# Attention sum of a graph network: one operand of the VectorE comparison is read from a bank of TensorE's memory

## The reference

```python
hp = jnp.einsum('nf,hfo->hno', h, w)
e = a_src[:, src] + a_dst[:, dst] + fc_b[0]
e = jax.nn.leaky_relu(e, negative_slope=0.2)
seg_max = jax.ops.segment_max(e.T, src, num_segments=n)
e = jnp.exp(e - seg_max.T[:, src])
seg_sum = jax.ops.segment_sum(e.T, src, num_segments=n)
att = e / seg_sum.T[:, src]
msg = att[:, :, None] * hp[:, dst, :]
agg = jax.vmap(lambda m: jax.ops.segment_sum(m, src, num_segments=n))(msg)
out = agg.mean(axis=0) + bias
```

## Time and profile before

| | |
|---|---|
| median of three runs | 31319.55 us (31306.85 to 31346.87) |
| profiled execution, its own time | 31347.26 us |
| its span | 31345.4 us |
| the stage's loop in it | 18986.3 to 21439.9 us, first to last start of `onehot` |
| busy in the loop (18986 to 21440 us) | PE 1739.85, DVE 2330.63, ACT 495.32, POOL 915.55 us |
| TensorE's granted clock in the loop | 0.62 of full speed (1.0 is 2.4 GHz, 0.5 is 1.2 GHz) |

### The profile page before, as it was taken

The page is one execution under the profiler, slowest core; times in us unless marked ns, Lnnn a source line. Parts: engine busy times, 40 slices in busy tenths (PEclk is TensorE's granted clock), DMA queues, the critical chain, the costliest instruction groups (busy, mean ns, idle before and its releaser), DMA issues. The chain is left out here.

```text
span 31345.4 us, 606960 instructions
## 1 busy us (share of the span) xinstructions
PE 25548.6 (82%) x149627; PEld 16798.5 (54%) x149628; DVE 18784.1 (60%) x47074; ACT 4500.2 (14%) x12240; POOL 16699.4 (53%) x16857
## 2 busy tenths in 40 slices
PE   8777776666678888858999986675888888888888
PEld 6444442222248888826777766664444444444444
DVE  9211115666653333325666668997777777777777
ACT  4111111111110000011111111221111111111111
POOL 0677777777767777716777763332333333333332
PEclk9555555555555555556665565656999999999999
DMA  2111112222221111113333355443332333333222
GB/s 65 34 30 30 30 30 50 51 51 50 51 38 25 25 25 25 25 14 74 79 79 77 80 71 107 124 124 81 70 71 70 71 70 71 71 71 72 71 70 64
DMA packets 2615644, 1869.03 MB, mean 60 GB/s; under 512 B 1600556, under 2 KB 2081066, under 8 KB 2613815
## 3 DMA queue, kind: packets, MB, share of 16 engines
q1 hardware_dynamic: 1914438, 1424.41, 18.6%
q0 software_dynamic: 516000, 217.22, 6.8%
q10 hardware_dynamic: 184400, 220.54, 2.8%
HBM read 1621.01 MB, written 238.82 MB: 59 GB/s over the span
## 5 line engine op out<-in xcount | busy, mean ns | idle before, releaser
L2027 POOL DMA_INDIRECT rows_x<-x_table,index x3125 | 3022.1, 967 | 6780.0 <-DMA index<-in_src 6018.0
L1295 POOL DMA_INDIRECT rows<-x_table,index x3625 | 3445.4, 950 | 2025.7 <-issue 1254.1
L162 PE MATMUL banks<-rows,onehot 128*128 128x33 f32 (+1 forms) x14440 | 3417.0, 413 | 1058.5 <-issue 586.6
L547 POOL DMA_INDIRECT rows<-x_table,index x3125 | 3021.7, 967 | 1853.5 <-DMA index<-in_src 927.2
L162 PEld LDWEIGHTS banks<-rows,onehot 128*128 128x128 f32 x14440 | 3186.1, 328 | 1366.1 <-issue 1357.0
L905 POOL DMA_INDIRECT bucket_pairs<-pair,place_int x3125 | 3150.0, 1008 | 1275.6 <-issue 1213.5
L696 POOL DMA_INDIRECT rows<-x_table,index x3125 | 3142.5, 1006 | 1019.6 <-issue 952.0
L1891 PE MATMUL banks<-first,same_unit 128*128 128x384 f32 (+1 forms) x10000 | 3503.3, 476 | 0.0
L1205 DVE CUSTOM_DVE_ANT_0 junk<-banks,mask 128x320 f32<-128x320 f32 x5800 | 2551.1, 486 | 1563.1 <-PE banks L1240 1540.7
L1760 DVE TENSOR_TENSOR second<-banks,h 128x384 f32<-128x384 f32 (+1 forms) x5000 | 2309.6, 485 | 1068.7 <-PE banks L1891 1015.0
L1879 PE MATMUL banks<-u_turned,w_tensor 32*128 32x384 f32 (+1 forms) x10000 | 2119.5, 501 | 530.9 <-DVE first L1752 530.7
(11 more groups left out here) (395 smaller groups left out, 39498.7 us busy)
## 6 DMA issues: line engine op xcount, KB each, us to landing
key_row<-key_rows SPq DMA_DIRECT2D x1450, 320.0 KB
h<-hidden_dram SPq DMA_DIRECT2D x10000, 40.0 KB
key_row<-dst_rows SPq DMA_DIRECT2D x625, 320.0 KB, 3.4
rows<-x_table,index POOLq DMA_INDIRECT x9875
a_dram<-a ACTq DMA_DIRECT2D x625, 160.0 KB
a<-a_dram SPq DMA_DIRECT2D x625, 160.0 KB
rows_dram<-rows ACTq DMA_DIRECT2D x725, 90.0 KB
x_rows<-rows_dram SPq DMA_DIRECT2D x725, 90.0 KB
```

The costliest lines, as they stand in the source:

```text
L162: mm = nc.tensor.matmul(m["ps"][7][:, 0:width], m["onehot"][j % 3][:, t * P:(t + 1) * P], rows[:, t, :], start=t == 0, stop=t == T - 1)
L547: nc.gpsimd.indirect_dma_start(out=m["rows"][j][:, t * W:t * W + F], out_offset=None, in_=m["x_table"], in_offset=bass.IndirectOffsetOnAxi ...
L1295: nc.gpsimd.indirect_dma_start(out=m["rows"][j][:, t * XA:t * XA + F], out_offset=None, in_=m["x_table"], in_offset=bass.IndirectOffsetOnA ...
L2027: nc.gpsimd.indirect_dma_start(out=m["rows_x"][j][:, t * F:(t + 1) * F], out_offset=None, in_=m["x_table"], in_offset=bass.IndirectOffsetO ...
```

## The change

A copy of the table `ramp` is made once, at the stage's start, in the first 128 columns of bank 3. The comparison of L1339 reads this copy and no longer the one in SBUF. Its other operand, `keys`, and its output stay in SBUF. No instruction moves.

```diff
+    ramp = lambda: m["ps"][3][:, 0:P]
+
...
     def hot_dve(dve, i, j):
         g = SLOTS * i + j
-        nc.vector.tensor_tensor(cut(m["onehot"][j][:, :], t=T), rep(m["keys"][:, bass.ds(T * g, T)], 2, P), rep(m["ramp"][:, :], 1, T),
+        nc.vector.tensor_tensor(cut(m["onehot"][j][:, :], t=T), rep(m["keys"][:, bass.ds(T * g, T)], 2, P), rep(ramp(), 1, T),
                                 ALU.is_equal).then_inc(s["hot"], 1)
...
             link = Chain(dve, s["step"])
             link(nc.vector.memset(m["acc"][:, :], 0.0))
+            link(nc.vector.tensor_copy(ramp(), m["ramp"][:, :]))
```

## The result

The changed kernel takes 30640 us in the median of four runs (30599.45 to 30681.72), the kernel before, on the same chip, 31331 us (31306.85 to 31346.87): a ratio of 0.978 (95% interval 0.9763 to 0.9797), 2.2% faster. The forecast was 30650 us. The profiled execution took 31345.4 us of span before and 30629.5 after, 715.9 us less. Of these the attention sum's loop gives 2453.6 - 1771.9 = 681.7 us (forecast 670); the loop began 18986.3 - 18932.8 = 53.5 us earlier and what lies behind it took 19.3 us more (9924.8 in place of 9905.5), in code that is the same; no run here explains these two, and single executions of the changed kernel lie up to 82 us apart.

A forecast was written before the change was run, and what follows sets the result against it. VectorE, busy 95% of the attention sum's loop, was taken as the bound. 2454 - 626 - 149 + 7 + 98 = 1784 us for the loop, a saving of 670, gave 30650 us in all; range 30530 to 30930.

The forecast's parts named there:

- The wait and its size: Attention sum's loop: the comparison `onehot` stops waiting for GpSimd's multiply in four groups of five, 580 x 1.08 = 626 us saved.
- Rival B: A comparison with one operand in a bank is still kept waiting; nothing changes, 31320 us; chance 0.06.
- rival C: The bank can't be read at speed beside TensorE's writes; `onehot` stretches, costing 341 us: 31660 us; chance 0.02.
- The price of the bank: Reading one operand of the comparison from a PSUM bank: 817 ns against 809, 7 us in all.
- `hot_turned`'s meetings: At the loop's end `hot_turned` would start 0.4 us ahead of GpSimd's multiply and no longer meet it: 149 us saved.
- VectorE's floor: VectorE's period for an ordinary group falls from 3.32 to 2.24 us and remains the bound at 2.4 GHz.
- The clock: TensorE's clock in the loop mostly raised, a quarter of the groups at the lower level: 98 us, bounds 0 and 392.
- (a): The two-operand addition L1369 slips by behind GpSimd's multiply with 0.03 us; at most 36 us, taken as 0.
- (b): TensorE's chain over two groups: 2.78 us a group at the lower clock, 2.19 at the higher, just below VectorE's 2.24.
- Rival A: TensorE stays at the lower clock and its chain becomes the bound: saving of 380, 30940 us; chance 0.18.
- (c): Transfers in the loop would hold 65% of the DMA engines, needed four groups later, over 9 us; cost taken as 0.
- D: Key rows come late, so `hot_turned` meets the multiply in each group (+1.05) and eats the gain: 31320 us; chance 0.02.

The follow-up runs named there:

- the swap: The changed kernel with the comparison's two operands exchanged (table in the bank first, keys in SBUF second): 36399 us, ratio 0.9815 to the kernel before.
- the memset: The kernel before with GpSimd's multiply done for one column in five, the other four filled by a memset: 36150 us (one run), loop 1975.8 us.

## Why the prediction was right

- **The wait and its size.** 580 x 1.08 = 626 us for the comparison: shown. Bank against SBUF, each alone in one edit, gives 0.81 and 1.89 us, and the swap and the memset show what is shared: GpSimd's reading against VectorE's second SBUF operand. Rival B and rival C are out.
- **The price of the bank.** Forecast 7 us, measured about none: 812 ns in the median, as in the 144 comparisons that didn't wait in the kernel before, and 809 at least in both. The rule of 62 more cycles (Trainium skill, "VectorE: DVE Perf Modes", the TRN2 errata), an estimate of 47 us, doesn't show in this instruction, which has one operand in each memory.
- **`hot_turned`'s meetings.** 149 us were booked on an argument about ScalarE's lateness. All 142 went, and came back when the lateness was removed. It was the boldest term and it carried, with less room than forecast: `hot_turned` led the multiply by 0.25 us (19703.72 and 19703.97), not 0.4, since the exponential started 0.12 us behind the start of ScalarE's copy (19703.56 and 19703.68) and did not wait for its end.
- **VectorE's floor.** Forecast 2.24 for an ordinary group, measured 2.23 (comparison to comparison, 19709.96 to 19712.19) to 2.29 (19699.25 to 19701.54). A turn at full clock is 1701.7 / 724 x 5 = 11.75 us, where the terms give 4 x 2.24 + 2.24 + 0.34 = 11.54. The 0.2 missing: behind a branch the sum starts 0.87 us after the comparison (19704.19 to 19705.06) and not 0.73 (19701.54 to 19702.27), 0.14 us a turn. In the kernel before it is 0.74 there (20207.86 to 20208.60): the long `hot_turned` ahead of it had covered the rest. That is 20 of the 30 us that the turns' difference makes over 145. The other 10 are an overlap of 0.07 us a turn: in other groups `hot_turned` starts 0.07 us before the last addition ends (19701.07 and 19701.14), behind a branch it starts 0.33 after it, and the terms count 0.34.
- **The clock.** A quarter of the groups at 1.2 GHz, 98 us, was a choice between 0 and 392; it measured 71. This term was the weakest, and it held by luck as much as by reasoning: TensorE was expected busier and so at the higher level, but it is busy 68% of the loop at 0.92 (1210.61 of 1773 us), less than the 71% at 0.62 of before.
- **(a) and (b)** stand as written: `L1371` slips by with 0.03 us, and TensorE's chain is the bound as soon as the clock is low (shown with the multiply doubled, 3.45 us measured for 3.39 a group). Rival A's mechanism, in the stretches at 1.2 GHz alone, is what the 71 us are.
- **(c)** Transfers hold 56% of the DMA engines (65% expected); `hot_turned` never waited for a key row, so D is out.

With the measured sizes the terms give 2453.6 - 626 - 149 + 71 + 30 = 1780, for 1771.9 measured; the forecast had 1784. So the mechanism was right, and that the sum came this close is luck in part: the 27 us too much for the clock and the 7 for the bank make up for the 30 that the turn's terms lack. The same holds for the whole: of the 46 us by which the profiled execution beat its forecast of 30677 (it took 30631) 12 come from the loop and 34 from code that is the same, and the median of the runs lies 9 us above that execution and not 28 below it.

## What to carry to other kernels

An instruction that takes twice its time in four cases of five is waiting inside its own busy time: compare its minimum with its median before calling an engine full. If GpSimd reads SBUF meanwhile, one of VectorE's two operands in a PSUM bank frees it, in either place, and for this float32 comparison at no price that counts (812 to 817 ns, against 812 unheld in SBUF). Then look for the next instruction with two SBUF operands, and for anything (a table load, a branch) that decides which of the two engines comes first: here 1.28 us of needless work a turn is worth more than it costs.

## What had not been expected of the hardware

- A one-operand float32-to-bf16 comparison waits for GpSimd's memset, which the two-operand one doesn't: 1255 ns at most, where 0.40 us of multiply and 0.53 of memset followed each other.
- GpSimd pays when it is second: 1.42 us in place of 1.27 behind `hot_turned`, as 1.52 behind the comparison in SBUF.
- A loop body of 55 groups costs VectorE 5.6 us of standing still at each return, in the mean of twelve; one of 10 groups had no pause before `hot_turned` over 0.33 us.
- The same program takes 30640 us on one chip and 36401 on another, with the same time in this loop. In the profile of the slower one the waits are longer in the stages with gathers, as in this pair (first the faster chip's, then the slower's):

```profile
L1295 POOL DMA_INDIRECT rows<-x_table,index x3625 | 3456.8, 954 | 1997.6 <-issue 1237.4
```
```profile
L1295 POOL DMA_INDIRECT rows<-x_table,index x3625 | 3441.2, 949 | 4282.2 <-issue 2959.9
```
